# The second of two weight blocks quantised in one expert tile is transposed behind the down-projection

## The reference

```python
for e in range(E):
    g = hs @ gate_proj[e].T
    u = hs @ up_proj[e].T
    inter = jax.nn.silu(g) * u
    out = out + comb[:, e:e + 1] * (inter @ down_proj[e].T)
...
wdq = (jnp.clip(jnp.round(wr / scale), -8, 7) * scale).reshape(shp)
...
q = (blocks / scales[..., None]).astype(jnp.float8_e4m3fn).astype(jnp.float32)
return (q * scales[..., None]).reshape(rows, feat)
```

## Time and profile before

| | us |
|---|---|
| runs | 4213.58, 4200.72, 4215.24 |
| median | 4213.58 |
| profiled execution, its own time | 4204.48 |
| span of its instructions | 4202.6 |
| mean granted clock of TensorE | 0.909 of full speed |

### The profile page before, as it was taken

How to read it: one execution, slowest core, us unless ns; L and a number is a source line. 1 busy time by engine, 2 the same in 40 slices (tenths; PEclk the granted TensorE clock), 3 DMA queues, 4 the chain that set the end, 5 groups by cost and what they waited for, 6 DMA issues and landing times.

```text
span 4202.6 us, 38866 instructions
## 1 busy us (share of the span) xinstructions
PE 3598.4 (86%) x13526; PEld 2246.8 (53%) x13526; DVE 2610.6 (62%) x3722; ACT 1197.0 (28%) x1974; POOL 524.1 (12%) x419
## 2 busy tenths in 40 slices
PE   2887877878787999999999959898989898989988
PEld 1653644544545676676767725643564346434743
DVE  5876877877855556767776534464447444744463
ACT  1332432332313444333333322212221232113210
POOL 1002003012021111111111021120111011101100
PEclk9988988889898999999999978899889987998799
DMA  4212202202107676766666540122011300221011
GB/s 144 61 32 59 72 18 59 72 17 71 38 13 233 227 232 203 233 216 216 227 221 218 189 170 30 71 89 96 30 70 66 120 30 36 95 105 50 1 60 40
DMA packets 277843, 444.62 MB, mean 106 GB/s; under 512 B 52560, under 2 KB 189776, under 8 KB 265104
## 3 DMA queue, kind: packets, MB, share of 16 engines
q1 hardware_dynamic: 256768, 383.74, 27.8%
q0 software_dynamic: 20880, 58.40, 4.2%
HBM read 368.49 MB, written 97.70 MB: 111 GB/s over the span
## 4 chain that ended last, share of the span: by engine, by line
PE 62%; DVE 22%; DVEq 5%; ACT 4%; issue 3%; DMA 2%; POOL 1%; SPq 0%; ACTq 0%; POOLq 0%
PE bank L969 14%; PE bank L980 8%; PE bank L1211 5%; PE bank L1224 4%; PE bank L1230 4%; PE bank L787 3%; PE bank L1119 3%; PE bank L1078 3%; DVE sb_gla L1790 2%; PE bank L1097 2%; DVE sb_ratio L1765 2%; DVEq L1771 2%; PE bank L1155 1%; PE bank L767 1%; PE bank L764 1%
## 5 line engine op out<-in xcount | busy, mean ns | idle before, releaser
L969 PE MATMUL bank<-sb_xT,sb_work 128*128 128x256 f32 x3024 | 665.3, 380 | 1.6 <-issue 0.8
L969 PEld LDWEIGHTS bank<-sb_xT,sb_work 128*128 128x128 f32 x3024 | 576.0, 191 | 106.8 <-issue 31.3
L787 PE MATMUL bank<-sb_gla,sb_work 128*128 128x256 f32 x896 | 260.6, 444 | 113.9 <-DVE sb_work L1792 101.1
L980 PE MATMUL bank<-sb_work,sb_hT 128*128 128x512 f32 x756 | 355.4, 622 | 0.0
L787 PEld LDWEIGHTS bank<-sb_gla,sb_work 128*128 128x128 f32 x896 | 189.5, 219 | 176.9 <-DVE sb_work L1792 122.3
L767 PE MATMUL bank<-sb_hT,sb_work 128*128 128x512 f32 x384 | 182.0, 622 | 100.6 <-DVE sb_hT L1739 100.6
L1592 POOL DMA_INDIRECT sb_parts<-scratch_h,sb_small x126 | 140.7, 1117 | 982.8 <-DMA sb_small<-scratch_ids 963.3
L1224 PE MATMUL bank<-sb_parts,sb_small 128*128 128x512 f32 x512 | 244.2, 622 | 4.5 <-ACT sb_small L1536 4.5
L1230 PE MATMUL bank<-sb_parts,sb_small 128*128 128x512 f32 x512 | 230.8, 593 | 5.9 <-DVE sb_work L2303 5.9
L980 PEld LDWEIGHTS bank<-sb_work,sb_hT 128*128 128x128 f32 x756 | 147.7, 202 | 164.2 <-issue 164.2
L1211 PE MATMUL bank<-sb_work,sb_parts 128*128 128x512 f32 x512 | 232.7, 614 | 2.7 <-ACT sb_work L1547 2.7
(11 more groups left out here) (363 smaller groups left out, 6059.0 us busy)
## 6 DMA issues: line engine op xcount, KB each, us to landing
sb_work<-scratch_gu SPq DMA_DIRECT2D x63, 1408.0 KB, 7.7
sb_parts<-scratch_mx SPq DMA_DIRECT2D x16, 3072.0 KB, 10.2
sb_work<-moe_w SPq DMA_DIRECT2D x63, 512.0 KB, 5.1
scratch_y<-sb_work SPq DMA_DIRECT2D x63, 512.0 KB, 6.7
sb_parts<-scratch_fq SPq DMA_DIRECT2D x24, 1024.0 KB, 6.9
sb_work<-w_qkvg SPq DMA_DIRECT2D x64, 256.0 KB, 2.6
scratch_gu<-moe_w SPq DMA_DIRECT2D x32, 512.0 KB, 5.7
sb_parts<-fT SPq DMA_DIRECT2D x48, 256.0 KB
```

The costliest lines, as they stand in the source:

```text
L787: mm = pe.matmul(dst.rearrange("p (h n l) -> p h n l", h=HPC, l=size), kS[u % 2][:, k * P:(k + 1) * P], late[:, :, k, :, 1, :], start=True ...
L969: mm = pe.matmul(dst, egu[j % 3][:, which * NC + k, m * P:(m + 1) * P], xt[j % 2][:, k, :], start=(k == 0), stop=(k == NC - 1))
L980: mm = pe.matmul(bank(YB[s]), einter[j % 2][:, m * SLOTS + s * P:m * SLOTS + (s + 1) * P], edn[j % 3][:, m * D:(m + 1) * D], start=(m == 0 ...
```

## The change

In tiles with two blocks, PE transposes the first where it did, and the second behind the down-projection. ScalarE likewise copies the first where it did, and the second behind `expert_y`. With one block nothing moves. SP, VectorE and GpSimd keep their order.

```diff
@@ tensor engine, loop over the expert tiles
                 if j + 1 < NTL:
                     expert_x(j + 1)
-                for i in prep_tiles(j - 1):
+                for i in prep_tiles(j - 1)[:1]:
                     prep_transpose(i)
                 if j:
                     expert_down(j - 1)
+                for i in prep_tiles(j - 1)[1:]:
+                    prep_transpose(i)
@@ scalar engine, the same loop
+            def prep_out(i):
+                act.wait_ge(prep_t.sem, i + 1)
+                if i >= 2:
+                    act.wait_ge(prep_st[i % 2].sem, 16 * (i // 2))
+                act.activation(pt_[i % 2], bank(7), ACT.Copy).then_inc(prep_c.sem, 1)
...
-                for i in prep_tiles(j - 1):
-                    act.wait_ge(prep_t.sem, i + 1)
-                    if i >= 2:
-                        act.wait_ge(prep_st[i % 2].sem, 16 * (i // 2))
-                    act.activation(pt_[i % 2], bank(7), ACT.Copy).then_inc(prep_c.sem, 1)
+                for i in prep_tiles(j - 1)[:1]:
+                    prep_out(i)
                 if j:
                     expert_y(j - 1)
+                for i in prep_tiles(j - 1)[1:]:
+                    prep_out(i)
```

## The result

| | before | with the change |
|---|---|---|
| median of the runs, us | 4209.4 (4 runs, 4200.7 to 4215.2) | 4136.9 (4 runs, 4128.9 to 4144.0) |
| profiled execution, span, us | 4202.6 | 4127.0 |
| mean granted clock | 0.909 | 0.917 |

The ratio is 0.983, with a 95% interval of 0.981 to 0.985: 72.5 us less by the medians. The forecast was 4141 us, with a range of 4122 to 4166. One more run of the kernel before (4205.2 us) has joined the three shown above, hence the other median. The change was timed twice more, at later times, with 0.982 (0.981 to 0.984) and 0.984 (0.982 to 0.986).

What follows compares the result with a forecast made beforehand. It took TensorE to bound the expert stage, stopping in 14 two-block tiles for ScalarE's copy. Stops cost 77.2 us, 10.5 stays, so 66.7 us comes off the 4208.5 mean: 4141 us, range 4122 to 4166.

Steps and rivals of the forecast that it cites:

- What bounds the stage: Expert stage: TensorE busy 1097.5 of 1176.6 us, its second block stopping 14 times, 47.4 us, for ScalarE's copy of the first.
- 77.2 us as the whole cost of the stops: The 14 two-block tiles took 319.15 us against 241.9 without stops: 50.8 idle, 26.4 busy but slower.
- The 10.5 us that stay: Two heavy two-block tiles keep four stops, 6.7 us, plus a clock loss of 1.9 us in each.
- The Trainium skill's rule: Clock halves only after a whole idle window running free of the program; remaining short stops then cost no clock, 4137 us.
- VectorE: It loses the pauses for catching up and runs 0.9 us late into the next tile; taken as nothing, at most 13 us.
- ScalarE, SP: Second copy done about 1.4 us after the tile's end, ahead of ScalarE's next work and SP's store; cost nothing.
- The sum: 77.2 - 10.5 = 66.7 us less, taken from the 4208.5 us mean: 4141 us.
- That the clock would not come back: Rival: the stops go but slow stretches occur anyway; gain 44.1 us, to 4160 us. Chance 0.10.
- That VectorE takes over: Rival: blocks get ready late more often, TensorE's transposes wait up to 13 us more for VectorE; 4155 us. Chance 0.12.
- That the stop only moves: Rival: the second block waits as long in its new place, ahead of the gate matmuls; 4200 to 4213 us. Chance 0.03.
- That steady work brings the clock down: Rival: through the expert stage the clock falls because TensorE no longer pauses; slower, 4230 us. Chance 0.02.

Runs made afterwards that it cites:

- TensorE's part alone: Against the kernel before, only TensorE's second-block transposes go behind the down-projection, ScalarE keeps its old order; ratio 0.984, 4144.9 us against 4216.6.
- ScalarE's part alone: Against the kernel before, only ScalarE's second-block copy goes behind the down-projection's evacuation, TensorE keeps its old order; ratio 1.000, 4215.1 us against 4216.6.
- earlier copy: Kernel before, TensorE's order unchanged; in double tiles ScalarE copies the first block ahead of the table load and exponential; ratio 0.988, 4162.0 us against 4216.6.
- half the cover: Changed kernel with the second block between the halves of the down-projection, its copy between the two evacuations; ratio 0.987, 4160.3 us against 4216.6 before.
- longer stop: Kernel before, with ScalarE copying the first block of each double tile three times over; ratio 1.007, 4239.6 us against 4211.8.
- planned kernel: Changed kernel with another block table: none in tiles with three VectorE ratio steps, two only in tiles with one; 0.981 of before twice, 4126.8 and 4134.5 us.
- planned blocks with the old order: Kernel before, its order kept, with a block table giving 18 double tiles instead of 14; ratio 0.999, 4205.9 us against 4211.8.

## Why the prediction was right

**What bounds the stage.** Right. TensorE set the pace. Taking away 44.6 us of its waits for the copy shortened the stage, and only 1.5 us of other waits took their place. That the copy's place behind the second block's transposes is the cause is shown from three sides: TensorE's part alone has the whole gain, ScalarE's alone has none, and an earlier copy, half the cover and a longer stop move the time by what they do to the stop.

**77.2 us as the whole cost of the stops.** Right in its parts. The step that the sum hung on was a double tile of 17.28 us; 12 took 17.26 (17.25 to 17.26 in every profile of the change). The 14 together took 248.66 us instead of 319.15, 70.5 less.

**The 10.5 us that stay.** Too high, by 3.8 us of it. For the two heavy tiles the prediction had stops of 1.7 and 1.6 us for the copy; they were 1.49 and 1.33, as these rows of the changed kernel show for the second one, with the tile behind it:

```profile
2116.31 0.66 PE L989 MATMUL bank<-sb_const,sb_parts 128*128 128x128 f32 x4 [2.41 <-DVE sb_parts L2081]
2116.80 5.32 PE L980 MATMUL bank<-sb_work,sb_hT 128*128 128x512 f32 x12
2123.45 0.63 PE L989 MATMUL bank<-sb_const,sb_parts 128*128 128x128 f32 x4 [1.33 <-ACT sb_parts L1438]
...
2136.81 0.66 PE L989 MATMUL bank<-sb_const,sb_parts 128*128 128x128 f32 x4 [1.50 <-DVE sb_parts L2081]
```

The clock loss of 1.9 us in each, the upper of two bounds, did not occur: the tiles took 20.14 and 21.41 us at clock 1.00. Against that, the four stops cost 0.2 us of refilling each (17.67 busy against 17.26), which the 10.5 did not hold. The Trainium skill's rule, weighed there ("TensorE: Matmul & The Clock Gate", Part 1), gave this result, 4137, and for stops of 0.88 us (13 in the runs with a short stop and before) and of 1.3 to 1.5 us, which cost no clock in any profile, the trace agrees. For longer ones it does not, and the measurement decides. Read with the page's own figure, the rule would also have spared the stops of 2.82 us, of which the one at 1370.03 cost 1.9 us; that it "fits" them, as the prediction says, holds only for their coming out either way.

The absence of the loss was in part luck. The first stop of the second heavy tile, 2.41 or 2.42 us in all nine profiles that have it, brought the slow clock in three: before, with ScalarE's part alone (0.88) and between the halves (0.99). In the other six, the three of the change among them, the block behind it took 0.66 us.

**VectorE.** Taken as nothing, with 13 us as its most. It cost 1.7 us, in a place that the prediction had not looked at: the tile behind the second heavy one, the last row above, 18.55 us instead of 16.82. VectorE ended its work of the heavy tile as late as ever, TensorE came 6.8 us sooner to the next (the double tile took 21.41 us instead of 28.24), and found the block not ready. The pauses were what VectorE caught up in, as the prediction said, but only where it was far behind. Behind ordinary double tiles nothing showed. Its waits for line 969 fell from 246.0 to 173.5 us, 72.5 less where 67 was written.

**ScalarE, SP.** Right. The second copy ended 1.29 us behind the down-projection, where 1.4 was the estimate, and so 0.85 us into the next tile. TensorE's part alone shows that 0.9 us more of lateness is free (there its last evacuation ended 1.77 us into the next tile). SP's queue never waited for the copy in the stage; behind this tile it issued the two blocks' stores at 1393.18, 6.2 us after the copy had ended.

**The sum.** In the profile: 70.5 in the double tiles, 1.7 for the clock of the single heavy tile, which came by itself, less 1.7 for VectorE, and 0.17 at the first tile: 70.6 us, and 66.7 forecast. The remaining 5 us of the profiled difference lie outside the stage, within what that part varies by from profile to profile. The forecast took 66.7 from 4208.5, which is 4141.8 and was given as 4141; that the median came within 5 us of it is in part luck, with a scatter of that size outside the stage.

**The rivals.** That the clock would not come back: refuted by 1.00 over the stage. That VectorE takes over: 1.5 us of it. That the stop only moves: 2 of 14 did, in part. That steady work brings the clock down: in the planned kernel TensorE's mean clock was 1.00 over 1047.8 us with 2.3 us of idle time. On this chip with one core there is no sign of it.

## What to carry to other kernels

A stop that one engine makes for another's short step, on its way to work that needs neither, is removed by exchanging the two, and the gain is the stop, up to the duration of what is put into it, and what the clock had lost with it: here 3.06 us a stop on average, and about 1.7 us more in slow matmuls behind it. Price the two separately. A stop up to 1.5 us cost its length and 0.2 us of refilling only, so shortening it (an earlier copy, 54.6 us) had three quarters of the gain of removing it (72.5 us); by the stage it was 49.1 of 70.6. Then look at who used the pauses. The engine next in load, VectorE here, is late first behind its heaviest pieces, and a table that keeps riders away from those took another 12 to 13 us off the stage.

## What the runs showed of the hardware

Whether a stop of TensorE of 2.4 to 3.3 us brings the half-rate clock is not decided by its length. Of stops of 2.8 to 3.3 us in ordinary double tiles, 10 of 11 did in the kernel before, 9 of 11 with ScalarE's part alone, and 9 of 18 in the planned blocks with the old order; the loss was 1.4 to 3 us where it occurred. Of stops of 2.41 or 2.42 us at one and the same place, 3 of 9 did. The only one of 2.21 us, in the run with the longer stop, did, with 1.9 us (clock 0.92). Stops up to 1.5 us never did, and stops of 4.15 and 4.67 us did in 11 of 11 tiles, with 1.9 to 3.1 us. That the middle lengths come out either way is what one part of a rule of the Trainium skill ("TensorE: Matmul & The Clock Gate", Part 1), a window that runs free of the program, would give. Its other part, that the whole window has to be idle, does not fit with the page's own figure: by it these stops alone would all have been spared. The measurement decides, and no run here shows where the window's borders lie.

The part of the program behind the expert stage takes 1781.8 to 1797.7 us in profiles of one and the same kernel, with TensorE's busy time moving by 15.5 us for the same matmuls; the part ahead of it takes 1282.5 to 1291.6. The three medians of the change, 4132.2 to 4151.9 us, scatter by about as much; that their scatter comes from these parts is shown for the profiled executions alone, whose stages agree within 0.5 us. A gain of 5 us is better read from the stage than from the total.
